# Last layer of a four-layer graph network: the destination rows of the 24 border tiles come from one-hot products on TensorE instead of from gathers by GpSimd

## The reference

```
s_n, v_n = equiv_layernorm(s, v, gamma_s, beta_s, gamma_v)
msg_s = (s_n @ Ws_src)[src] + (s_n @ Ws_dst)[dst]
msg_v = einsum('ncx,cd->ndx', v_n, Wv_src)[src] + einsum('ncx,cd->ndx', v_n, Wv_dst)[dst]
w1 = rbf @ W_rbf
m1_s, m1_v = cg_tp(msg_s, msg_v, y0, y1, w1[...])
a = leaky(m1_s @ W_alpha) . alpha_dot          # softmax over the edges of a destination
h = ...(products of m1, gates, a second cg_tp) # one row of 160 for each edge
out = node + segment_sum(alpha * h, dst) @ Wp
```

## Time and profile before

| what | value |
|---|---|
| median of 3 runs | 7282.01 us (7276.09 to 7289.44) |
| the profiled execution's own time | 7280.35 us |
| its span in the profile | 7278.6 us |
| PE busy, share of the span | 6735.4 us, 93% |
| DVE busy | 6241.9 us, 86% |
| ACT busy | 3802.7 us, 52% |
| POOL busy | 4946.0 us, 68% |
| granted TensorE clock, mean | 0.946 of full speed |

### The profile page before, as it was taken

One profiled execution on the slowest core, in us unless ns is written; L12 is line 12 of the kernel. 1 busy time (PEld: TensorE's weight loads), 2 busy tenths in 40 slices (PEclk: granted clock), 3 DMA queues, 4 the chain that ended last, 5 costly groups with the idle time before them and its releaser, 6 DMA issues. The chain is left out here.

```text
span 7278.6 us, 114637 instructions
## 1 busy us (share of the span) xinstructions
PE 6735.4 (93%) x33428; PEld 4526.3 (62%) x33428; DVE 6241.9 (86%) x17139; ACT 3802.7 (52%) x10244; POOL 4946.0 (68%) x3534
## 2 busy tenths in 40 slices
PE   6999999997899999989999983999999999998488
PEld 3445444444555555645555551888888888887376
DVE  6999999996698888778888872999999999998794
ACT  3555455553333333433333331777777777776485
POOL 2887888884377777547777734888888888885000
PEclk7999999997799999989999995999999999999797
DMA  8999999998222222112222212444444444443363
GB/s 230 175 176 177 174 178 175 175 177 188 70 65 64 65 66 65 48 51 68 68 69 69 69 35 67 90 96 98 98 95 95 96 94 97 94 97 75 100 192 97
DMA packets 551879, 778.19 MB, mean 107 GB/s; under 512 B 94113, under 2 KB 402630, under 8 KB 551014
## 3 DMA queue, kind: packets, MB, share of 16 engines
q0 software_dynamic: 323136, 419.33, 34.7%
q1 hardware_dynamic: 223894, 350.90, 15.9%
q10 hardware_dynamic: 4240, 0.64, 0.1%
HBM read 469.60 MB, written 300.92 MB: 106 GB/s over the span
## 5 line engine op out<-in xcount | busy, mean ns | idle before, releaser
L678 POOL DMA_INDIRECT fore<-node_table,src_i x1664 | 1714.5, 1030 | 647.1 <-issue 501.1
L1629 DVE TENSOR_TENSOR work<-work 128x384 f32<-128x384 f32 (+5 forms) x4912 | 1998.1, 433 | 54.1 <-DMA work<-src_sum 26.7
L792 POOL DMA_INDIRECT fore<-src_table,put_i x784 | 1592.4, 2031 | 242.4 <-issue 234.4
L745 POOL DMA_INDIRECT src_sum<-work,put_i x808 | 1294.6, 1602 | 396.4 <-issue 174.5
L1381 PE MATMUL bank<-work 128*128 128x384 f32 (+1 forms) x3328 | 1201.3, 504 | 14.4 <-DVE work L1629 14.4
L1381 PEld LDWEIGHTS bank<-work 128*128 128x128 f32 x3328 | 604.2, 191 | 693.4 <-issue 311.4
L951 ACT ACTIVATE work<-bank 64x512 f32<-64x512 f32 x416 | 245.8, 591 | 1434.7 <-PE bank L1348 1434.6
L1629 DVE TENSOR_TENSOR work<-work,bank 128x384 f32 (+6 forms) x2068 | 891.6, 431 | 80.2 <-issue 70.5
L1333 PE MATMUL bank<-work 128*128 128x480 f32 x1616 | 750.3, 598 | 2.2 <-DVE work L1629 1.9
L1362 PEld LDWEIGHTS bank<-w_fc,work 64*128 64x128 f32 x3328 | 532.7, 188 | 238.1 <-issue 225.9
L1479 PE MATMUL bank<-ident,work 128*128 128x128 f32 x4704 | 650.8, 275 | 26.6 <-DVE work L1629 25.1
(11 more groups left out here) (274 smaller groups left out, 12744.4 us busy)
## 6 DMA issues: line engine op xcount, KB each, us to landing
edge_h<-work SPq DMA_DIRECT2D x196, 320.0 KB
work<-edge_h SPq DMA_DIRECT2D x196, 320.0 KB, 3.4
work<-keys SPq DMA_DIRECT2D x196, 256.0 KB, 6.2
fore<-in_dst_row SPq DMA_DIRECT2D x196, 256.0 KB, 4.3
fore<-node_table,src_i POOLq DMA_INDIRECT x1664, 2.7
work<-in_edge_attr SPq DMA_DIRECT2D x196, 128.0 KB, 6.1
src_sum<-work SPq DMA_DIRECT2D x4, 6240.0 KB, 37.6
work<-src_sum SPq DMA_DIRECT2D x100, 240.0 KB, 4.3
```

Source lines behind the costliest of these rows:

```text
L678: return pool.indirect_dma_start(dst, None, table, bass.IndirectOffsetOnAxis(ap=idx, axis=0), bounds_check=bound, oob_is_err=True)
L745: pool.indirect_dma_start(src_sum[t], bass.IndirectOffsetOnAxis(ap=put_i[:, e:e + 1], axis=0), E.run[:, g % 2, t * 480:(t + 1) * 480], Non ...
L792: pool.indirect_dma_start(T.rows[:, b, t, :], None, src_table, bass.IndirectOffsetOnAxis(ap=put_i[:, e:e + 1], axis=0), compute_op=ALU.add ...
L1629: return V_.tensor_tensor(o, p, q, op)
```

## The change

POOL gathers only the source rows of the border tiles, in three parts of 10, 10 and 4 tiles, each with its own semaphore (`border_in`). The destination rows are made like those of the other tiles. SP loads the numbers of the border tiles into registers, and with 24 DMAs at addresses from these registers loads the destination numbers of each border tile, as 16-bit integers, to all partitions (`T.border_keys`). DVE makes 24 matrices of zeros and ones from them. PE multiplies matrix k with window k + 1 of `skip`. ACT copies the products out, three tiles at a time. DVE adds them to the gathered source rows, in the three parts, and SP writes each part to `src_table`.

Since the buffers for this take more room, `T.turns` is laid ahead of the region that is shared. SP keeps one set of 24 registers instead of two: it loads `tile_i` or `unit_i` again at each place where it needs the other, once fewer ahead of the first layer, once more behind the first layer's edges, once ahead of the border tiles, once more ahead of the second pass.

```diff
+PARTS = ((0, 10), (10, 20), (20, MORE))
...
-            v.border = work[:, at_f:at_f + MORE * DIM].rearrange("p (k c) -> p k c", c=DIM)
+
+            b = carve()
+            b(at_f)
+            v.border, v.border_dst, v.border_turned = b(MORE, DIM), b(MORE, DIM), b(MORE, P)
+            v.border_keys = b(MORE * P // 2).bitcast(I16).rearrange("p (k n) -> p k n", n=P)
...
             barrier(sp, "sp")
-            more = [sp.alloc_register(f"sp_unit{k}") for k in range(MORE)]
-            sp.load(more, unit_i[0:1, 0:MORE])
-            more = [sp.snap(r, donate=True, min_val=0, max_val=UNITS - 1) for r in more]
-            more_tiles = [sp.alloc_register(f"sp_tile{k}") for k in range(MORE)]
-            sp.load(more_tiles, tile_i[0:1, 0:MORE])
-            more_tiles = [sp.snap(r, donate=True, min_val=0, max_val=TILES - 1) for r in more_tiles]
+            at_borders = [sp.alloc_register(f"sp_border{k}") for k in range(MORE)]
+
+            def border_tile(k):
+                return sp.snap(at_borders[k], min_val=0, max_val=TILES - 1)
...
+            sp.load(at_borders, tile_i[0:1, 0:MORE])
...
             unrolled(FIRST_GROUPS, [(-2, edge_keys), (0, edge_scalars)])
             barrier(sp, "sp")
+            sp.load(at_borders, unit_i[0:1, 0:MORE])
             unrolled(SLOTS, [(0, sums_in)])
...
+                sp.load(at_borders, tile_i[0:1, 0:MORE])
+                for k in range(MORE):
+                    tile = border_tile(k)
+                    sp.dma_start(T.border_keys[:, k, :], keys16.rearrange("(e w n) -> w e n", w=2, n=P)[1][bass.ds(tile, 1), :]
+                                 .rearrange("o n -> (o n)").partition_broadcast(P)).then_inc(s.border_keys_in, 16)
                 for g in range(2):
                     dst_keys(g)
                     rbf(g)
-
-                sp.wait_ge(s.border_rows, 16 * MORE)
-                sp.dma_start(src_table[ROWS:ROWS + MORE * P].rearrange("(k p) c -> p k c", p=P), T.border).then_inc(s.border_kept, 16)
+                for i, (k0, k1) in enumerate(PARTS):
+
+                    sp.wait_ge(s.border_added, i + 1)
+                    sp.dma_start(src_table[ROWS + k0 * P:ROWS + k1 * P].rearrange("(k p) c -> p k c", p=P),
+                                 T.border[:, k0:k1]).then_inc(s.border_kept, 16)
...
+                sp.load(at_borders, unit_i[0:1, 0:MORE])
                 halves = edge_h.rearrange("(g p h t) f -> g p h (t f)", h=2, t=2, p=P)
...
-                for k in range(MORE):
-                    gather(T.border[:, k, :], src_table[0:ROWS], border_src_i[:, k:k + 1], last_row).then_inc(s.border_src_in, 16)
-
-                pool.wait_ge(s.border_src_in, 16 * MORE)
-                for k in range(MORE):
-                    pool.indirect_dma_start(T.border[:, k, :], None, dst_table, bass.IndirectOffsetOnAxis(ap=border_dst_i[:, k:k + 1], axis=0),
-                                            compute_op=ALU.add, bounds_check=last_row, oob_is_err=True).then_inc(s.border_rows, 16)
-
-                pool.wait_ge(s.border_kept, 16)
+                for i, (k0, k1) in enumerate(PARTS):
+                    for k in range(k0, k1):
+                        gather(T.border[:, k, :], src_table[0:ROWS], border_src_i[:, k:k + 1], last_row).then_inc(border_in[i], 16)
+
+                pool.wait_ge(s.border_kept, 16 * len(PARTS))
...
+                for i in range(MORE // 3):
+
+                    act.wait_ge(s.border_mm, 3 * i + 3)
+                    act.activation(T.border_dst[:, 3 * i:3 * i + 3, :].rearrange("p k c -> p (k c)"), bank[:, i, 0:3 * DIM],
+                                   ACT.Copy).then_inc(s.border_rows_out, 1)
...
+                for k in range(MORE):
+
+                    pe.wait_ge(s.border_turned, k + 1)
+                    nc.tensor.matmul(bank[:, k // 3, k % 3 * DIM:(k % 3 + 1) * DIM], T.border_turned[:, k, :], skip[:, k + 1, 0:DIM],
+                                     start=True, stop=True).then_inc(s.border_mm, 1)
+
+                pe.wait_ge(s.border_rows_out, MORE // 3)
...
+                def border_rows():
+
+                    for i, (k0, k1) in enumerate(PARTS):
+
+                        dve.wait_ge(border_in[i], 16 * (k1 - k0))
+
+                        dve.wait_ge(s.border_rows_out, -(-k1 // 3))
+                        tt(T.border[:, k0:k1], T.border[:, k0:k1], T.border_dst[:, k0:k1], ALU.add).then_inc(s.border_added, 1)
+
                 def first_turned(g):
+                    if g == 2:
+                        border_rows()
...
+                dve.wait_ge(s.border_keys_in, 16 * MORE)
+                for k in range(MORE):
+                    V_.tensor_scalar(T.border_turned[:, k, :], T.border_keys[:, k, :], place[:, TILES + k:TILES + k + 1], None,
+                                     ALU.is_equal).then_inc(s.border_turned, 1)
```

More of the change, by code:

```diff
@@ L258, in build @@
         put = [sem(f"put{c}") for c in range(CHAINS)]
+        border_in = [sem(f"border_in{i}") for i in range(len(PARTS))]
         s = type("Signals", (), one)
@@ L335, in l3_views @@
             v.cv = g(2, GROUP, 196)
+            v.turns = g(3, GROUP, 9)
             at_f = g.used()
             v.f, v.f2 = g(2, GROUP, 352), g(2, GROUP, 352)
-            v.border = work[:, at_f:at_f + MORE * DIM].rearrange("p (k c) -> p k c", c=DIM)
+            b = carve()
+            b(at_f)
+            v.border, v.border_dst, v.border_turned = b(MORE, DIM), b(MORE, DIM), b(MORE, P)
+            v.border_keys = b(MORE * P // 2).bitcast(I16).rearrange("p (k n) -> p k n", n=P)
             v.t1, v.t2 = g(2, 2, 384), g(2, 2, 384)
@@ L344, in l3_views @@
             v.nine = g(GROUP, 9, V)
-            v.turns = g(3, GROUP, 9)
             v.h = g(2, GROUP, DIM)
@@ L539, in edge_scalars @@
                     for t in range(GROUP):
-                        tile = more_tiles[GROUP * (g - GROUPS) + t]
+                        tile = border_tile(GROUP * (g - GROUPS) + t)
                         sp.dma_start(E.attr[0:64, b, t * P:(t + 1) * P],
@@ L574, in stage @@
                         for i in range(2):
-                            unit = more[2 * (g - GROUPS) + i]
+                            unit = border_unit(2 * (g - GROUPS) + i)
                             sp.dma_start(W.attr[0:k, b, i * 256:(i + 1) * 256],
```

4 lines of the change are left out of this document (3 added, 1 removed).

## The result

| | before | after |
|---|---|---|
| median, us (lowest to highest, runs) | 7279.1 (7276.09 to 7289.44, 4) | 7224.64 (7219.53 to 7230.45, 4) |
| profiled execution, span, us | 7278.6 | 7219.1 |
| first border gather, us | 4444.46 | 4454.99 |
| head: from there to the pass's first gather | 88.2 | 41.1 |
| pass: from there to SP's first load behind it | 2175.4 | 2153.0 |

The ratio is 0.9922, with a 95% interval from 0.9906 to 0.9937: faster, by 54.5 us between the medians. The span became 59.5 us shorter: 47.1 in the head and 22.4 in the pass, less 10.5 by which the border stage began later; the last 0.5 lie behind the pass.

What follows compares the result with a forecast made beforehand. The prediction took POOL's back-to-back gathers to bound the pass, behind an 88 us head with POOL alone busy. 7280.35 - 48.4 (POOL's earlier start) + 0 (register loads) = 7232, stated as 7234 for the median; range 7222 to 7250.

Steps and rivals of the forecast that it cites:

- Keys: SP's 24 key transfers for the border tiles: 0.48 us each, 11.6 us, then 4.2 us of landing.
- rivals of 1.08 us and of serial transfers: SP's key transfers at 1.08 us each, time 7248, 10%; or each behind the last one's landing, time 7319, 3%.
- PE's 24 products, 17.2 us: PE's border products at the half-clock price of 0.715 us each, the 24th done at 4478.8.
- clock rises, gathers set the end: Rival for the border stage: PE reaches full clock and gathers end last; gain 50.6 us, time 7231, 25%.
- The gathers' chain, "unchanged": POOL's 24 border source gathers all landed at 4477.67, as before the change.
- a quarter more on ten gathers, 2.5 us: Rule weighed: gathers behind 4461, beside a busy DVE, a quarter longer, so the chain ends 2.5 us later, at 4480.2.
- My own sign of being wrong: In the border stage, a source gather taking over 1.2 us while DVE works would show the forecast wrong.
- POOL is held up by DVE: Rival: gathers shut out during each DVE comparison, 6.2 us in all; gain 44.4 us, time 7238, 8%.
- Tail: Writes of parts two and three, 14 of 24 tiles: 5.1 us from 4479.2, so POOL starts at 4484.3.
- Carry-over, one for one: If POOL starts the pass x us earlier, the pass ends x us earlier; rival that it does not: 7269, 4%.
- The distance to the end of the pass as before: From POOL's first fourth-tile gather to the pass's end takes as long as before; everything behind is earlier by one constant.
- Register loads, net 0: SP's register loads, one fewer before layer 0's edges, more later: together 0, between -0.5 and +2 us.

Runs made afterwards that it cites:

- r_after: The changed kernel run again on another chip, nothing else changed; ratio to the kernel before 0.9922, head 45.7 us, pass 2150.9 us.
- experiment 5: The two runs e_pad_60 (61 tiny DVE writes in the kernel before) and e_drop_pad (31 in e_drop's kernel); ratios 0.9971 and 0.9915.
- r_before: The kernel before run again on another chip, nothing changed; ratio 0.9998, head 88.3 us, pass 2182.4 us.
- e_turns: The kernel before with only the tile T.turns laid where the change lays it; ratio to before 1.0001, pass 2167.8 us.
- e_drop: The kernel before without the 24 adding gathers, nothing in their place; ratio to before 0.9942, head 41.8 us, pass 2187.4 us.
- e_drop_pad: The kernel before without the 24 adding gathers and with 31 tiny DVE writes ahead of the pass; ratio to before 0.9915.
- e_pad_after: The changed kernel with 98 tiny DVE writes ahead of the border comparisons; ratio to the kernel before 0.9948, head 52.1 us, pass 2171.2 us.
- e_pad_before: The kernel before with 31 tiny DVE writes ahead of the pass, making DVE's program 30 instructions longer; ratio to before 0.9977.
- e_pad_60: The kernel before with 61 tiny DVE writes ahead of the pass, making DVE's program 60 instructions longer; ratio to before 0.9971.
- e_longer: The changed kernel with 24 more source gathers on POOL ahead of the pass, and a wait for them; ratio to the kernel before 0.9967.
- e_late_adds: The changed kernel with DVE waiting for all three parts of the gathered rows before its first add; ratio to the kernel before 0.9919.
- a_kept_later: The changed kernel with POOL's wait for the border rows moved behind the pass's first two destination gathers; ratio to the kernel before 0.9930.

## Why the prediction was right, and where it was not

7234 was forecast and 7224.64 came, faster and inside the range. The mechanism was right for the head: the adding gathers go, POOL starts that much earlier, and the pass carries it through. The head's gain of 48.4 us was 47.1, but of its terms two were off by more than 4 us, in opposite senses, and the chain that set the end was the other one. That the sum came out is in part luck. All from the barrier gather on:

| step | forecast | after |
|---|---|---|
| keys landed | 16.7 | 20.0 |
| last product copied | 35.0 | 30.8 |
| gathers landed | 33.2 | 37.4 |
| POOL's first gather of the pass | 39.8 | 41.1 |

- *Keys:* the price of 0.48 us for each was nearly right (12.65 us for 24, 0.53 each in after, 0.58 in r_after), which ends the rivals of 1.08 us and of serial transfers. The last landed in 5.8 us instead of 4.2.
- *PE's 24 products, 17.2 us:* mis-sized, 9.79 us. I had taken the half-clock row because PE had stood idle. The stretches below (PE, PEld, DVE, ACT, POOL: busy us and instructions; then the granted clock) have no PE work and 0.50 up to 4475, and 0.70 on average over the 11 us of the products. PE worked without a gap from 4475.43 on, and from 4482 to 4486 the clock is 1.00. The rival *clock rises, gathers set the end*, 25%, is the one that happened in mechanism; its gain of 50.6 us was missed because the gathers had become longer.

```profile
4455.00:4475.00 20.00, 0.00 (x0) 0.00 (x0) 0.01 (x1) 0.00 (x0) 15.42 (x16) 0.50 0.44 101
4475.00:4486.00 11.00, 9.79 (x48) 9.58 (x48) 8.67 (x32) 4.57 (x8) 8.87 (x8) 0.70 0.38 113
4482.00:4486.00 4.00, 3.22 (x24) 2.98 (x22) 2.71 (x2) 2.85 (x5) 3.39 (x3) 1.00 0.27 74
4486.00:4496.00 10.00, 5.29 (x16) 3.57 (x16) 1.77 (x2) 1.62 (x5) 2.84 (x2) 0.62 0.74 220
```

- *The gathers' chain, "unchanged":* this step failed. It was 4.2 us longer. The two long gathers make 2.6 of it and a longer landing most of the rest (3.2 us behind the last gather's end, where the earlier trace rows have 1.9). I had weighed a quarter more on ten gathers, 2.5 us, and dropped it on a row with a comparison beside it. The comparisons did cost only 0.06 us for each of a few gathers; the adds, which have two inputs, I never priced by themselves. My own sign of being wrong, a source gather of over 1.2 us while DVE works, came true with them. No run shows the 6.2 us of the rival *POOL is held up by DVE*, gathers held up for as long as each comparison runs: beside the 24 comparisons they took 1.01 to 1.07 us, and beside two of the adds 2.50 and 2.14.
- *Tail:* one write behind the last add, 2.9 us from its end to POOL's start, where I had 5.1 for two. With the gathers last, the two other writes had been issued before, and only one was left to wait for.
- *Carry-over, one for one:* right for the head (45.6 of 46.5 us in experiment 5). "The distance to the end of the pass as before" was wrong: 22.4 us shorter. This is the step that failed in mechanism. I had read the earlier trace rows as one steady state, POOL back to back, with nothing done ahead that could wait in store. It is an average over two rhythms, and in the short one POOL has up to 7.7 us of gathers in store. A mean of 2031 ns between 1732 and some 2050, and starts of m1's products taken in stretches of eight, would have shown the break at group 64.
- *Register loads, net 0:* PE's first product of layer 0 came 3.0 us earlier than before, the sums' first transfer 2.1 later, and layer 1's table 0.6 later: nothing that counts, as forecast.

So luck had its part in the total too. With the 22.4 us of the pass included the forecast would have been 7212 and below all that was measured: the medians differ by 54.5 us, not by 47.1 + 22.4. In the profiled execution 10.0 us of the difference went into a longer layer 1; what the other executions do in layer 1 and in the pass is not recorded. On the other chips the pass varies from 2167.8 to 2187.4 us among r_before, e_turns and e_drop, which have the same DVE program, while the six profiles in the short rhythm lie within 1.8 us of each other. So part of the gain probably depends on when an execution of before slips. By the ratios the two parts come out apart: the head alone 0.9942 (e_drop), the place alone 0.9977 and 0.9971, both together 0.9915 (e_drop_pad) and 0.9922 (the change).

## What to carry to other kernels

Where two chains run into one wait, price the later one beside the work of the other: the gathers were "unchanged" in the code, and two of them took 2.6 us longer together beside the adds. Before calling a loop of hundreds of groups steady, take its period in stretches, and the lead of each engine that works ahead of another; a mean can hide two rhythms, and then a change that puts instructions ahead of the loop can be faster or slower for that alone. So when a result is off by a few tenths of a per cent, run the kernel before with as many idle instructions as the change adds: here that told 0.25% of place from 0.6% of work.

## What the runs showed of the hardware

- In before, r_before, e_turns and e_pad_after DVE pauses 0.23 to 0.28 us ahead of m1's first product once in 128 instructions, as long as the short rhythm lasts, and a packet of 8.2 KB on the instruction queue follows within 2 us. Moving the loop by 30 (r_after, e_pad_before) or by 60 instructions (e_pad_60) took this pause away, and moving it by 128 (e_pad_after) brought it back, at 0.25 to 0.28 us. In e_drop, at before's place, it is not seen.
- In e_pad_after DVE's 98 writes of one column, 0.06 us each, did not run back to back: they came in groups of 1 to 23 with 0.25 to 1.36 us between them (8.4 us in 11 pauses), while SP's transfers at run-time addresses took 29.76 us for 24, and 13.87 in r_after. The 31 writes of e_pad_before had one pause, of 0.2 us, and the 61 of e_pad_60 three, 1.2 us together. Whether both are one cause was not tried.
- A gather of 128 rows took 1.01 us on POOL beside an idle DVE (before and after), 1.01 (before), 1.06 to 1.07 (after, r_after) and at most 1.14 (e_longer) beside comparisons of 128x128, and 2.14 and 2.50 beside adds of 128x1600 (after). In the pass it took 2.50 at most where the short rhythm lasts throughout (after), and up to 3.65 in before and 3.80 in e_drop and e_longer.
- In four kernels on the other chips (r_after, e_longer, e_late_adds, a_kept_later) ACT stood idle for 6.6 to 7.9 us between its second and third copy behind the barrier, though PE had gone on. In after's first profile and in e_pad_after it did not happen.
